# A second mask sum in its own bank, x ahead of a gate weight, and the gate rows' copies shared between two engines

## What is computed

```python
mod = (silu(c) @ wmod).reshape(2, 6, 1, 512)      # shift, scale, gate, twice
sa, ca, ga, sb, cb, gb = mod[:, 0], ..., mod[:, 5]
ga, gb = sign(g) * max(|g|, 0.25) of each         # the gates
h = layernorm(x) * (1 + ca) + sa
w = weight * (its 32x32 block of the mask has a one)
x = x + ga * (h @ w.T + bias)                     # first half, "attention"
h = layernorm(x) * (1 + cb) + sb
x = x + gb * (w2'(silu(w1' h) * (w3' h)))         # second half; w' = w + 2 b a, hidden width 1376
```

## Time and profile before

| | |
|---|---|
| time, median of 3 runs | 252.25 us (252.08 to 252.29) |
| time of the profiled execution | 252.32 us |
| its span, first to last instruction | 250.5 us |
| TensorE busy | 242.3 us (97%), clock granted in full throughout |
| VectorE busy | 135.9 us (54%) |
| ScalarE busy | 89.6 us (36%) |
| GpSimd busy | 97.3 us (39%) |
| chain that ended last: TensorE, VectorE | 82%, 6% of the span |

### The profile page before, as it was taken

The page is one execution under the profiler, slowest core; times in us unless marked ns, Lnnn a source line. Parts: engine busy times, 40 slices in busy tenths (PEclk is TensorE's granted clock), DMA queues, the critical chain, the costliest instruction groups (busy, mean ns, idle before and its releaser), DMA issues.

```text
span 250.5 us, 3526 instructions
## 1 busy us (share of the span) xinstructions
PE 242.3 (97%) x1265; PEld 192.8 (77%) x1265; DVE 135.9 (54%) x221; ACT 89.6 (36%) x151; POOL 97.3 (39%) x102
## 2 busy tenths in 40 slices
PE   7799999899999999999999999999999999999993
PEld 6677768787788888888888778888888888888772
DVE  2847899899999744744754631741233123312224
ACT  2376554843324465465422311122112221222110
POOL 1377492326532131230210351497346435643300
PEclk9999999999999999999999999999999999999999
DMA  6999991023224413213217520030000000000005
GB/s 184 345 384 407 413 401 42 3 84 119 51 84 127 126 47 123 84 42 128 84 46 107 45 13 0 38 132 0 0 0 4 0 0 0 4 0 0 0 0 169
DMA packets 13041, 24.02 MB, mean 96 GB/s; under 512 B 1240, under 2 KB 2648, under 8 KB 13024
## 3 DMA queue, kind: packets, MB, share of 16 engines
q1 hardware_dynamic: 12864, 23.65, 30.2%
q10 hardware_dynamic: 160, 0.15, 0.2%
HBM read 21.18 MB, written 2.10 MB: 93 GB/s over the span
## 4 chain that ended last, share of the span: by engine, by line
PE 82%; DVE 6%; DMA 3%; issue 3%; POOL 2%; ACT 1%; SPq 1%; DVEq 0%; POOLq 0%; ACTq 0%
PE up_b L1156 25%; PE up_a L1156 24%; PE acc L1170 8%; PE acc L1171 8%; PE acc L1169 8%; DMA wmod_sb<-in_wmod 3%; PE side L1137 2%; DVE xt L839 1%; DVE stats L699 1%; PE acc L999 1%; DVE wa L813 1%; PE side L1141 1%; DVE xt L818 1%; PE acc L1106 1%; POOL ht_lo L419 1%
## 5 line engine op out<-in xcount | busy, mean ns | idle before, releaser
L940 DVE TENSOR_TENSOR g<-up_b,g 128x512 f32<-128x512 f32 (+1 forms) x22 | 15.2, 690 | 64.5 <-PE up_b L1156 64.5
L1170 PE MATMUL acc<-w_lo,g_hi 128*128 128x512 f32 (+1 forms) x88 | 34.7, 394 | 0.0
L1171 PE MATMUL acc<-w_hi,g_lo 128*128 128x512 f32 (+1 forms) x88 | 34.7, 394 | 0.0
L1169 PE MATMUL acc<-w_hi,g_hi 128*128 128x512 f32 (+1 forms) x88 | 34.6, 394 | 0.0
L670 ACT ACTIVATE g<-up_a 128x512 f32<-128x512 f32 (+1 forms) x22 | 13.1, 597 | 58.8 <-PE up_a L1156 58.5
L827 DVE SCALAR_TENSOR_TENSOR raw<-side,raw 128x512 f32<-128x512 f32 (+2 forms) x33 | 21.5, 676 | 22.3 <-PE side L1137 15.7
L677 ACT ACTIVATE g_hi<-g 128x512 fp32r<-128x512 f32 (+1 forms) x22 | 13.9, 633 | 49.4 <-DVE g L940 49.4
L462 POOL TENSOR_TENSOR w_lo<-work,w_hi 128x512 fp32r<-128x512 f32 (+1 forms) x11 | 14.2, 1287 | 41.1 <-ACT w_hi L604 41.1
L597 ACT ACTIVATE w_hi<-raw 128x512 fp32r<-128x512 f32 (+2 forms) x33 | 20.3, 626 | 21.2 <-DVE raw L827 21.1
L944 DVE TENSOR_TENSOR g_lo<-g,g_hi 128x512 fp32r<-128x512 f32 (+1 forms) x22 | 22.9, 1041 | 8.7 <-ACT g_hi L677 8.4
L1156 PE MATMUL up_a<-ht_hi,w_lo 128*128 128x512 f32 (+1 forms) x88 | 24.2, 396 | 0.4 <-DVE w_lo L833 0.4
(11 more groups left out here) (172 smaller groups left out, 379.3 us busy)
## 6 DMA issues: line engine op xcount, KB each, us to landing
raw<-in_ffn SPq DMA_DIRECT2D x33, 256.0 KB, 2.7
wmod_sb<-in_wmod SPq DMA_DIRECT2D x4, 1024.0 KB, 11.5
xt<-in_x SPq DMA_DIRECT2D x8, 256.0 KB, 8.2
wmod_sb<-in_wmod SPq DMA_DIRECT2D x1, 2048.0 KB, 15.1
out<-xt SPq DMA_DIRECT2D x8, 256.0 KB, 2.7
mask_sb<-in_mask SPq DMA_DIRECT2D x4, 256.0 KB, 9.2
wa<-in_weight SPq DMA_DIRECT2D x4, 256.0 KB, 9.2
lora_raw<-in_lora SPq DMA_DIRECT2D x1, 512.0 KB, 10.4
```

The costliest lines, as they stand in the source:

```text
L940: nc.vector.tensor_tensor(g[0:w], up_b[0:w], g[0:w], ALU.mult).then_inc(g_ready, 1)
L1169: nc.tensor.matmul(acc[t][:], hi, down_hi[j][0:w], start=(j == 0), stop=False)
L1170: nc.tensor.matmul(acc[t][:], hi, down_lo[j][0:w], start=False, stop=False)
L1171: last = nc.tensor.matmul(acc[t][:], lo, down_hi[j][0:w], start=False, stop=(j == HT - 1))
```

## The change

Six edits, all in the first 45 us of the program.

1. `mask_bank(1)` is `acc[3]` in place of `side[0]`. TensorE's list puts `attend_bias(0)` ahead of `mask_blocks(1)`, and `turn(3)`, which writes `acc[3]`, waits for `block_on_ready` 2 and goes ahead of `mod_products(0, 1)`; the places of `mask_blocks(2)` and `mask_blocks(3)` among the `attend` calls move back, `gate_rows(0)` by two calls, and `attend(0, 3, 0)` goes ahead of `gate_spread()`.
2. SP issues the second batch's four x tiles ahead of the gate's 1 MB of modulation weights.
3. VectorE takes `moment(4)` ahead of `mask_on(3)`, and `gates_of(0)` goes behind its two norms. On ScalarE `gate_size(0)` goes behind its two norms.
4. `gate_spread` runs over banks outside and batches inside, and signals each bank by itself. ScalarE copies the first and third bank, VectorE the second and fourth.
5. `lora_high(1)` and `lora_part(1)` come early: the latter right behind `lora_part(0)` and ahead of `whole(4)`, no longer behind `columns()`.
6. GpSimd takes the roots of the second batch first, then waits for `gates_ready`, and only then runs `low(3)` and `masked_weight_low(3)`, in this order.

```diff
-GATE_COPIES = T
+GATE_COPIES = T // 2
...
+        gate_row_by_act = sem("gate_row_by_act")
...
         def mask_bank(k):
-            return acc[1] if k >= 2 else side[0]
+            return (side[0], acc[3], acc[1], acc[1])[k]
...
+            load_x(1)
             load_mod(GATE_A, SHIFT_F, wmod_ga_loaded)
-            load_x(1)
...
             low(2)
-            masked_weight_low(3)
-            low(3)
             root(T, 2)
             root(T + 2, 2)
+
+            pool.wait_ge(gates_ready, 1)
+            low(3)
+            masked_weight_low(3)
             spread(0)
...
+            def gate_copy(q):
+
+                act.wait_ge(spread_out, TURN_BANKS.index(q) + 1)
+                act.wait_ge(block_on_ready, KT)
+                src = acc[q][:, 2 * P:(2 + B) * P].rearrange("p (b n) -> p b n", b=B)
+                nc.scalar.activation(mask_sb[:, 0:B, q * P:(q + 1) * P].bitcast(F32), src, ACT.Copy
+                                     ).then_inc(gate_row_by_act, 1)
...
             whole(3)
-            gate_size(0)
             norm(T)
             norm(T + 1)
+            gate_size(0)
             lora_high(0)
+            for q in TURN_BANKS[0::2]:
+                gate_copy(q)
+            lora_high(1)
             high(4)
...
-            for n in range(1, len(LORA_CUTS)):
+            for n in range(LORA_FIRST, len(LORA_CUTS)):
                 lora_high(n)
...
             def gate_copy(q):
 
-                dve.wait_ge(spread_out, 1)
+                dve.wait_ge(spread_out, TURN_BANKS.index(q) + 1)
...
                 dve.wait_ge(gate_row_ready, GATE_COPIES)
+                dve.wait_ge(gate_row_by_act, GATE_COPIES)
...
             mask_sum(3)
+            moment(4)
             mask_on(3)
             mask_weight(3)
-            moment(4)
             moment(5)
             moment(6)
             moment(7)
             centres(T)
-            gates_of(0)
             norm(T + 2)
             norm(T + 3)
-            for q in TURN_BANKS:
+            gates_of(0)
+            for q in TURN_BANKS[1::2]:
                 gate_copy(q)
             lora_part(0)
+            lora_part(1)
             whole(4)
...
             columns()
-            lora_part(1)
             centres(2 * T + 2)
...
-                    pe.wait_ge(gate_row_ready, k + 1)
+                    pe.wait_ge(gate_row_ready if k % 2 else gate_row_by_act, k // 2 + 1)
...
-                for b in range(B):
-                    for q in range(KT):
-                        rows = slice(q * QUAD, (q + 1) * QUAD)
+                for q in TURN_BANKS:
+                    rows = slice(q * QUAD, (q + 1) * QUAD)
+                    for b in range(B):
                         row = q * QUAD + b
...
-                last.then_inc(spread_out, 1)
+                    last.then_inc(spread_out, 1)
...
             fill(FILL_H)
-            mask_blocks(1)
             pe.wait_ge(ones_ready, 1)
             pe.wait_ge(bias_ready, 1)
             pe.wait_ge(cols_ready, 1)
+            pe.wait_ge(block_on_ready, 1)
+            attend_bias(0)
+            mask_blocks(1)
+            attend(0, 0, 0)
             pe.wait_ge(block_on_ready, 2)
-            attend_bias(0)
-            attend(0, 0, 0)
+            turn(3)
             mod_products(0, 1)
-            turn(3)
+            attend(0, 0, 1)
             mask_blocks(2)
-            attend(0, 0, 1)
             first_columns(1)
             attend(0, 0, 2)
-            mask_blocks(3)
             attend(0, 1, 0)
             attend(0, 1, 1)
+            mask_blocks(3)
             attend(0, 1, 2)
             attend(0, 2, 0)
-            gate_rows(0)
             attend(0, 2, 1)
             attend(0, 2, 2)
+            gate_rows(0)
+            attend(0, 3, 0)
             gate_spread()
-            attend(0, 3, 0)
             turn(4)
```

More of the change, by code:

```diff
@@ L1086, in attend_bias @@
                     pe.wait_ge(gate_row_ready, GATE_COPIES)
+                    pe.wait_ge(gate_row_by_act, GATE_COPIES)
                 for t in ts:
```

## The result

The changed kernel takes 252.72 us, the median of 7 runs (252.65 to 253.20); the kernel before took 252.13 us beside it (251.82 to 252.34, 7 runs). The ratio is 1.0028, with an interval of 1.0018 to 1.0037: **slower by 0.3%**. The profiled execution took 252.65 us, its span is 250.9 us, its mean granted clock 1.00.

The account below looks back on a forecast made before the run. TensorE, 97% busy, gains only where it stands still; its last restart, at 60.56 us, follows VectorE's list. 252.32 + 1.6 - 0.56 = 253.4, less 0.07 to the median: 253.3 us; own range 252.9 to 253.8, whole range 251.9 to 253.8.

Parts of the forecast that it names:

- Step 1: VectorE's second mask multiply comes 0.13 us too late behind GpSimd's low(0), waits its full hold, ends 1.54 us later.
- Rival A: VectorE's second mask multiply gets in ahead of GpSimd's low(0), without a hold; 252.4 us, no change; chance 0.25.
- Step 2: What hangs on the second multiply: whole(1) ends at 19.33 us, the third multiply, held by low(1), at 21.3, not 19.82.
- Step 3: Second batch's x lands at about 20.7 us, not 23.35; VectorE's moments end at about 26.3, against 26.69.
- Step 4: Norms, then gate on VectorE: norms 1.3 us behind moments, gates_ready at 29.1 us, not 27.89; copies end by about 31.0.
- Step 5: VectorE's LoRA parts partly held by GpSimd's low(3) and masked_weight_low(3); whole(4) starts 1.65 us later.
- Rival C: TensorE's gate spread gets long, 2.9 us at most instead of 0.73; 254.2 us; chance 0.08 together with Rival D.
- Rival B: On top of Rival A, the LoRA parts are not held by GpSimd's lows; 251.6 us, faster; chance 0.17.
- Step 6: GpSimd's first root step near 44 us no longer meets lora_part(1): 0.22 instead of 0.78 us, minus 0.56.
- Rival D: DMAs served side by side, so x lands hardly earlier; time like Rival C's; chance 0.08 together with Rival C.
- handed on: Lateness passed through GpSimd's lows and add_x1(0) to the second norm: 1.6 us.

Follow-up runs that it names:

- e7: The changed kernel with GpSimd waiting for the second mask multiply ahead of low(0) and the fourth ahead of low(2): 252.26 us, ratio 1.0000 to the kernel before.
- e6: The changed kernel without GpSimd's wait for gates_ready ahead of low(3): 255.59 us, ratio 1.0134 to the kernel before.
- e2: The changed kernel with lora_high(1) and lora_part(1) back at their old places: 253.04 us, ratio 1.0032 to the kernel before.
- e3: e1 with both LoRA parts ahead of the gate copies, GpSimd waiting for the parts, its spread(0) behind low(7): 253.00 us, scattered over 251.91 to 254.13.
- b0: The kernel before, unchanged, profiled a second time: 252.28 us.
- e5: e3 with GpSimd's low(2) waiting for the fourth mask multiply: 251.98 us, ratio 0.9989 to the kernel before.
- b1: The kernel before with only lora_high(1) and lora_part(1) moved early, behind lora_part(0): 252.14 us, ratio 0.9987 to the kernel before.
- e1: The changed kernel with TensorE's second mask sum back ahead of the bias: 252.99 us, ratio 1.0031 to the kernel before.
- e4: e1 with GpSimd's low(2) waiting for the fourth mask multiply: 252.01 us, ratio 0.9993 to the kernel before.
- e3 again: The same program as e3, run once more for its profile: 252.94 us.
- e8: e5 with the gate's weights loaded ahead of the second batch's x again: 254.44 us, ratio 1.0089 to the kernel before.
- b2: The kernel before with only the second batch's x loaded ahead of the gate's weights: 252.65 us, ratio 1.0013 to the kernel before.

## Why the prediction was right, point by point

- **Step 1, right.** Forecast: multiply at 15.47, 0.13 us behind `low(0)`, with a full hold. Measured: 0.16 us behind, 1.68 us long. Rival A (VectorE wins) is out, and e7 shows that this hold carries the slowdown. The Trainium skill (SBUF — State Buffer, "Who interferes with whom") says that whoever issues first has the shared ports for the whole instruction and the other is blocked fully. The runs agree down to 0.07 us: 0.24 and 0.25 us late (e6, e2) cost 0.90, 0.16 late 0.99, 0.10 late 1.04, 0.09 late 1.06, 0.07 late 1.90 over two operations, and 0.01 us early nothing. That 0.13 and 0.16 lie so close is partly luck: TensorE's filling products came 0.67 us earlier than the forecast had them and `low(0)` 0.58, and the comparison stood 0.43 us behind its mask sum, not 0.33; the two errors cancel.
- **Step 2, right in length**: the third multiply is held too (1.21 us; 1.15 before), the fourth no more than 0.02.
- **Step 3, right.** x costs no wait at 21.38 us. The moments end at 25.72, forecast 26.3. The cover of `gate_rows(0)` was over-sized, 1.2 us in the forecast: e3 and e7, with it in the same place, waited for its weights until 25.79 and 25.87 us, and after the change it starts at 26.08.
- **Step 4, right.** The norms follow the moments by 1.29 us (forecast 1.3), the copies end at 30.15. Rival C is out: the spread takes 0.75 us, against 0.73 in the old order. The Trainium skill (TensorE: Matmul & The Clock Gate, "Part 3: Packing small matmuls — row/col tiling") says that a weight load overlaps with running matmuls only when its row group differs. In the new order every second product has the row group of the one before it, and no cost of that can be seen in these 16.
- **Step 5, right.** The parts were held, 0.87 us; forecast was one partly covered hold, 0.9 us (32.8 against 31.9). Rival B is out. `low(7)` ends 0.92 us later, not 1.6, for the reason below.
- **Step 6, right.** 0.78 became 0.23: minus 0.55, forecast minus 0.56.
- **Rival D is out** with step 3.

**The step that was off is the base of step 1**, and through it the size of the sum. The forecast took 14.41 us and 15.34 us from one execution, and so carried its late start into the changed kernel: `low(0)` was to start at 15.34 and started at 14.76, 0.58 us earlier. Take 0.58 from every forecast that hangs on it, and the chain fits: gates 28.5 (28.53), `whole(4)` 32.2 (32.12). In the kernel before an earlier start did not count, as b0 shows. So the term "handed on" was 0.92 us in place of 1.6; less 0.55 is 0.37, and the restart moved by 0.39. By medians the change cost 0.59 us, where 1.04 was forecast. The two profiled executions differ by only 0.33 us; the other 0.26 are where they lie in their ranges, that of before 0.19 us above the median of its 7 runs, that of after 0.07 below.

So the mechanism was right point by point and the size too large. The measured 252.72 us lies under the forecast's own range (252.9 to 253.8) and just above rival A's (252.1 to 252.7), whose mechanism is refuted: it is inside the whole range because that had been widened for A.

**Left open**: what makes the slowest runs of e3, and whether a version clearly under the kernel before exists. e5 (0.9989, up to 1.0001) and b1 (0.9987, up to 0.9996) are the lowest here, both a tenth of a per cent. That the start made the difference of 0.58 us is read off profiles of several kernels; of the changed kernel itself only one exists.

## What to carry to other kernels

Where two engines exclude each other, look in the trace for pairs that start within some 0.2 us of each other: each such tie is worth nearly the whole operation that the loser waits for, here 1.0 of 1.3 us, and any edit ahead of it may flip it or move it to the next pair (e1). Decide it by a wait on the engine with slack (e4: 1 us gained by adding one), and before taking out a wait ask what it keeps apart (e6: 2.9 us lost). And take the base of a sum from what pins the chain: an edit that removes the pin, here a transfer, makes the jitter of the start count, so a time from one execution is no anchor.

## What the runs showed of the hardware that I had not expected

- VectorE's norm, an operation with one tile operand in SBUF, is held by GpSimd as fully as the multiplies with two: 2.90 us for two norms in e6, 1.00 alone. The prediction had counted only multiplies and LoRA parts, with two. A norm lasts 0.54 us where the moments' sum over the same 512 columns takes 0.68, and those moments are not held (0.68 at 23.21 us after, beside `low(2)` from 23.01). This agrees with the same section of the Trainium skill, by which an operation that goes over one tile with both ports contends as well.
- The hold works both ways and from the first hundredth: GpSimd's `low(2)` took 1.83 us in e3, 0.01 us behind VectorE, and 1.29 us in e3 again, 0.10 us ahead.
- In e6 the granted clock was at 0.50 for some 3 us after TensorE had stood for 2.23 and then 0.52 us; in the profiles of e8 (longest stop 1.09 us), e3 again (1.19), e1 (1.30) and b2 (1.34) it stayed at 1.00 there.
